# Adapter groups issued behind a quad's last product, and five steps of the start and of superblock 3 issued at other places

## What is computed

```python
scale = cond @ norm_w.T + 1.0
h = x * (scale[:, None, :] * rsqrt(mean(x * x) + 1e-6))
val, gate = split(h @ up_w.T, 2)                  # up_w 4096 x 512
h = val * gelu(gate)                              # exact gelu
y = act_quant(h) @ weight_quant(down_w).T         # 2048 -> 512, int8 steps per token
x = y + x
Wd_b = Wd + ((cond @ Wdd.T + bdd) * 0.1).reshape(B, 128, 512)
Wu_b = Wu + ((cond @ Wdu.T + bdu) * 0.1).reshape(B, 512, 128)
x = x + relu(x @ Wd_b.T + bd) @ Wu_b.T + bu
```

## Time and profile before

| | |
|---|---|
| median of 3 runs | 892.72 us (890.46 to 893.59) |
| profiled execution, its time | 893.21 us |
| its span, first to last instruction | 891.5 us |
| PE busy | 860.0 us, 96% |
| DVE, ACT, POOL busy | 68%, 43%, 8% |
| mean granted PE clock | 0.994 of full |
| DMA, mean | 206 GB/s |
| PE's share of the chain that ended last | 77%; DVE 8%, DMA 6%, ACT 3% |

### The profile page before, as it was taken

One profiled execution on the slowest core, in us unless ns is written; L12 is line 12 of the kernel. 1 busy time (PEld: TensorE's weight loads), 2 busy tenths in 40 slices (PEclk: granted clock), 3 DMA queues, 4 the chain that ended last, 5 costly groups with the idle time before them and its releaser, 6 DMA issues.

```text
span 891.5 us, 11928 instructions
## 1 busy us (share of the span) xinstructions
PE 860.0 (96%) x4026; PEld 375.0 (42%) x4026; DVE 607.7 (68%) x944; ACT 384.7 (43%) x630; POOL 70.2 (8%) x79
## 2 busy tenths in 40 slices
PE   6889999999999999999999999999999999999988
PEld 5233343344444434444434444444444444444433
DVE  5757667588888775546886664558885764435976
ACT  5467787566645452224545452215433332224000
POOL 0413123130200000000200000000200000001000
PEclk9989999999999999999999999999999999999999
DMA  9739887766779895547595585353546443432311
GB/s 351 271 128 305 312 304 227 285 217 215 267 262 329 295 322 195 201 147 254 204 319 199 201 297 179 123 175 99 176 130 202 143 163 121 146 112 71 141 71 71
DMA packets 64283, 183.50 MB, mean 206 GB/s; under 512 B 7008, under 2 KB 8032, under 8 KB 64224
## 3 DMA queue, kind: packets, MB, share of 16 engines
q1 hardware_dynamic: 63936, 182.48, 59.2%
q10 hardware_dynamic: 288, 0.26, 0.1%
HBM read 152.31 MB, written 29.36 MB: 204 GB/s over the span
## 4 chain that ended last, share of the span: by engine, by line
PE 77%; DVE 8%; DMA 6%; issue 3%; ACT 3%; SPq 1%; POOL 0%; DVEq 0%; ACTq 0%; POOLq 0%
PE aux_ps L1078 9%; PE b_ps L989 8%; PE b_ps L993 7%; PE b_ps L991 7%; PE aux_ps L1034 6%; PE a_ps L989 5%; PE a_ps L993 5%; PE a_ps L991 5%; DMA w_ring<-in_Wdd 5%; PE aux_ps L1140 3%; PE e_ps L989 3%; PE c_ps L989 3%; PE e_ps L991 3%; PE c_ps L993 3%; PE c_ps L991 3%
## 5 line engine op out<-in xcount | busy, mean ns | idle before, releaser
L786 ACT ACTIVATE b_ps<-a_ps 128x512 f32<-128x512 f32 x63 | 36.7, 582 | 178.9 <-PE a_ps L993 178.7
L1475 DVE SCALAR_TENSOR_TENSOR h_ring<-v_sb,unscale,gelu 128x512 f32<-128x512 f32 x63 | 48.6, 772 | 87.7 <-ACT gelu L810 55.2
L989 PE MATMUL b_ps<-t_mov,u_l 128*128 128x512 f16 x252 | 95.8, 380 | 2.1 <-DVE c_ps L1436 2.0
L993 PE MATMUL b_ps<-t_mov,u_l 128*128 128x512 f16 x252 | 95.5, 379 | 0.0
L991 PE MATMUL b_ps<-t_mov,u_l 128*128 128x512 f16 x252 | 95.5, 379 | 0.0
L1444 DVE TENSOR_TENSOR v_sb<-b_ps,p_sb 128x512 f32<-128x512 f32 x63 | 43.5, 690 | 66.0 <-PE b_ps L993 65.6
L1499 DVE TENSOR_TENSOR hmax<-gelu,hmax 128x512 f32<-128x512 f32 x120 | 82.4, 687 | 6.7 <-ACT gelu L816 1.1
L1078 PE MATMUL aux_ps<-h_ring,wq 128*128 128x512 f16 x384 | 84.8, 379 | 0.0
L1034 PE MATMUL aux_ps<-w_ring,cond_sb 128*32 128x512 f32 x480 | 69.2, 601 | 7.4 <-DMA w_ring<-in_Wdd 3.6
L681 POOL PARTITION_ALL_REDUCE yscale<-hmax x8 | 18.0, 2298 | 606.1 <-DVE hmax L1499 606.1
L820 ACT ACTIVATE gelu<-h_ring 128x512 f32<-128x512 f32 x64 | 40.3, 630 | 55.0 <-DVE h_ring L1475 55.0
(11 more groups left out here) (214 smaller groups left out, 1605.9 us busy)
## 6 DMA issues: line engine op xcount, KB each, us to landing
w_ring<-in_Wdu SPq DMA_DIRECT2D x64, 512.0 KB, 7.0
w_ring<-in_Wdd SPq DMA_DIRECT2D x56, 512.0 KB, 7.1
u_l<-ul_dram SPq DMA_DIRECT2D x48, 512.0 KB, 4.4
u_e<-ue_dram SPq DMA_DIRECT2D x48, 384.0 KB, 3.1
h_ring<-in_up_w SPq DMA_DIRECT2D x16, 512.0 KB, 6.9
x_sb<-in_x SPq DMA_DIRECT2D x8, 1024.0 KB, 8.4
res<-in_down_w SPq DMA_DIRECT2D x16, 512.0 KB, 6.0
ul_dram<-u_l SPq DMA_DIRECT2D x15, 512.0 KB, 7.8
```

Source lines behind the costliest of these rows:

```text
L989: pe.matmul(ps[:, :], weight(n, p, 0, k), hi, start=fresh and k == 0, stop=False, skip_group_check=True)
L993: mm = pe.matmul(ps[:, :], weight(n, p, 1, k), hi, start=False, stop=k == 1, skip_group_check=True)
L1475: dve.scalar_tensor_tensor(out=h_slot(n)[:, TB:TS], in0=val[:, :], scalar=unscale[:, s // 2, j:j + 1], in1=gelu2[:, :], op0=ALU.mult, op1= ...
```

## The change

Four things, none of which changes an operation; the same instructions are issued on each engine.

1. On PE the two adapter groups of a quad stand behind product 7, at the head of the side work.
2. In the start on DVE: `power(1)` directly behind `rsqrt(1)`, ahead of one low part of the weights, one of x and four `x_scaled`; the sum T4 ahead of `seed_c(1)` instead of behind `u_low(2, 0)`.
3. In the start on ACT: `u_high(1, 1)` and the copy of group 4 ahead of the high part of T3; the copies of groups 5, 6 and 7 each one step or more earlier; the row sums of chunk 4 at the end of the start instead of in the middle of quad 1.
4. In superblock 3 on DVE: `scales(3, 0)` in quad 50 ahead of `multiply2(49)` and `seed_c(50)`, instead of ahead of `val2(50)`.

```diff
--- before.py
+++ after.py
@@ -865,17 +865,18 @@
             t_high(0, T1)
             t_high(0, T2)
             u_high(1, 0)
+            u_high(1, 1)
+            stage_group(4)
             t_high(0, T3)
-            stage_group(4)
-            u_high(1, 1)
             gate2(0)
+            stage_group(5)
             u_high(1, 2)
+            stage_group(6)
             u_high(1, 3)
-            stage_group(5)
-            stage_group(6)
+            stage_group(7)
             absolute1(0)
             absolute2(0)
-            stage_group(7)
+            row_sums(4)
             for n in range(1, NQ):
                 s, j = divmod(n, NP)
                 last = j == NP - 1 and s + 1 < NSB
@@ -901,7 +902,7 @@
                     absolute2(n - 1)
                 if last:
                     t_high(s + 1, T2)
-                if s == 0 and j + 3 < NP:
+                if s == 0 and 1 < j and j + 3 < NP:
                     row_sums(j + 3)
                 if n > 1:
                     absolute1(n - 1)
@@ -1189,11 +1190,11 @@
                     if n > 1:
                         product(n - 1, 4)
                     product(n, 2)
-                    for g in groups_of_quad(n):
-                        adapter_group(g)
                     product(n, 7)
-                for key in side_work(n)[len(groups_of_quad(n)):]:
-                    if key[0] == "stat":
+                for key in side_work(n):
+                    if key[0] == "dw":
+                        adapter_group(key[1])
+                    elif key[0] == "stat":
                         stat(key[1])
                     elif key[0] == "rs":
                         spread_rs(key[1])
@@ -1615,10 +1616,10 @@
             x_scaled(0, (2, 3))
             mean_square(1)
             rsqrt(1)
+            power(1)
             u_low(0, 2)
             t_low(0, B21)
             x_scaled(1)
-            power(1)
             t_low(0, B12)
             t_low(0, B22)
             moving_sum(0, T1)
@@ -1635,6 +1636,7 @@
             t_low(0, T3)
             u_low(1, 2)
             u_low(1, 3)
+            moving_sum(0, T4)
             seed_c(1)
             running_max1(0)
             running_max2(0)
@@ -1671,6 +1673,8 @@
                         power(j + 2)
                     if j + 1 < NP:
                         u_low(j + 1, 0)
+                if s == NSB - 1 and j == 2:
+                    scales(s, 0)
                 if s > 0 and j in QUANTISE:
                     first = 1 + sum(v for q, v in QUANTISE.items() if q < j)
                     quantise(s - 1, range(first, first + QUANTISE[j]))
@@ -1679,9 +1683,7 @@
                 if last:
                     moving_sum(s + 1, T2)
                     t_low(s + 1, B11)
-                if n == 1:
-                    moving_sum(0, T4)
-                else:
+                if n > 1:
                     multiply2(n - 1)
                     seed_c(n)
                     multiply1(n - 1)
@@ -1698,8 +1700,10 @@
                     t_low(s, B22)
                 if j == 0 or n == 1:
                     t_low(s, T4)
-                if s > 0 and j in (1, 2):
-                    scales(s, 2 - j)
+                if s > 0 and j == 1:
+                    scales(s, 1)
+                if 0 < s < NSB - 1 and j == 2:
+                    scales(s, 0)
                 val2(n)
                 if n == 1:
                     sums_low(0)
```

## The result

| | before | after |
|---|---|---|
| median of the runs, us | 892.33 (888.31 to 893.59, 6 runs) | 877.18 (875.56 to 880.11, 6 runs) |
| profiled execution, us | 893.21 | 875.56 |
| its span, us | 891.5 | 873.8 |

The ratio is 0.984, 95% interval 0.9815 to 0.9866: the changed kernel is 1.6% faster. The prediction was 875.0 with a range of 870.5 to 883.5. The profiled pair shows 17.7 us.

The account below looks back on a forecast made before the run. PE's own matmuls bound the kernel; reordering returns only waits and lost clock. Start 8.5, superblock 0 6.0, quads 35 and 38 2.2, scales(3, 0) 1.3: 18.0 us off 893.2, given as 875, range 870.5 to 883.5.

Parts of the forecast that it names:

- The start, 8.5 forecast: Start to quad 3: reordered VectorE and ScalarE work makes quad 3 start about 9.2 us earlier, taken as 8.5.
- the wait for group 7's bank: Start: PE still waits 1.9 us for the copy of group 5, which frees that bank.
- the replay: Start recomputed at full clock from timeline durations: quad 3 starts near 65.3 to 66.3 us, against 75.21.
- The first rival: Start: the clock falls again behind remaining waits, up to 3.0 us of work lost, 877 to 878; chance 0.15.
- the sign that the clock is full from 24 us on: Start: listed among what would show the forecast right, full PE clock from 24 us on.
- Superblock 0, 6.0 forecast: Quads 4 to 14: product 7 runs during tile waits, 5 x 1.30 = 6.5 us, less 0.5 for bounds.
- the five quads of the forecast: Quads 4, 7, 9, 12 and 14 of superblock 0: each gains 1.30 us from groups behind product 7.
- a sign of being wrong: Groups behind product 7: the forecast is wrong if they still take 3 us there.
- Quads 35 and 38, 2.2 forecast: Tiles issued later behind a queue backlog land when they did, so the quads gain 0.93 + 1.30 = 2.2 us.
- scales(3, 0), 1.3 forecast: Quads 50 and 51: moved into VectorE's idle time, it removes product 7's seed wait in quad 51, 1.3 us.
- The spare of 0.5 in quad 17: Quad 17, second tightest: without the groups as cover, 0.5 us are left between seed end and product 7.
- The rival of a kernel that gets slower: 28 quads with groups: product 7 waits for a late seed, some 20 us lost or 903 us total; chance 0.03.

Follow-up runs that it names:

- the third part alone: Kernel before with only scales(3, 0) moved two products earlier: 889.46 us, ratio 0.9988 [0.9961, 1.0015].
- the late seed on before: Kernel before with multiply2 issued four times instead of once ahead of seed_c in twelve quads with groups: 897.76 us in its one run.
- the earlier issue: SyncE issues a quad's weight tiles one loop iteration earlier where the quad between has no groups: on the kernel before 887.74 us, on the changed kernel 874.12 us.
- the second part alone: Kernel before with only the adapter groups moved behind product 7, start and scales(3, 0) as before: 882.91 us, ratio 0.9905.
- the three kernels with other copies: Changed kernel with ScalarE's copies early and some groups in front: 877.44 us; with tiles also issued earlier 872.74; that at chosen quads only 874.22.
- the late seed: Changed kernel with multiply2 issued four times instead of once ahead of seed_c in twelve quads with groups: 888.65 us in its one run.

## Why the prediction was right, step by step

**The start, 8.5 forecast, 7.7 measured.** The mechanism held. Group 1 starts at 26.23 with no wait. The sum T3 runs from 40.03 to 41.24 (forecast: ends at 40.1). The seed's wait in quad 2 is 1.40 (1.6), that of the bounds 0.49 (0.4), and the wait for the row sums is gone. The mis-sized term is the wait for group 7's bank: 3.02, against 1.9. T3 ended 1.1 later than in the replay, and the copy that frees the bank stands behind T3's high part, which gives the difference. The replay took VectorE's durations from stretches in which GpSimd was idle; a later section shows what that missed. Quad 3 begins at 66.75 to 66.80 in the two traces of this start without a stretch at half the clock, and at 67.25 to 68.00 in the five with one; the replay had 65.3 to 66.3.

The first rival, the clock falling again, came true in part. It does so behind the wait of 3.02 and costs 0.7 in the profiled run, 0.5 to 1.2 over those traces; the rival had up to 3.0. So the sign that the clock is full from 24 us on failed. The median, 877.2, is the number of this rival (877 to 878), but not for its reason: the two of the six runs at a mean clock of 1.0 took 877.43 and 876.93, no less than the four at 0.998.

**How much of the 7.7 is clock.** The start of before, with no half-clock stretch (trace of the third part alone), reaches quad 3 at 71.69, and with the two of its own profile at 75.21. The changed start without one reaches it at 66.80. So the waits give 4.9, and the clock the other 2.8: 3.5 less 0.7. The forecast of 8.5 had the clock in it: it set a replay at full clock against a start that ran twice at half, and gave 3 us as the clock's part. The Trainium skill, TensorE: Matmul & The Clock Gate, Part 1, says that how many matmuls run slow at a kernel's start varies between runs of one kernel. These traces show such a difference later in the start too: quad 3 starts at 76.01, 75.21 and 71.69 in three traces whose code is the same up to there (the late seed on before, before, the third part alone).

**Superblock 0, 6.0 forecast, 7.7 in the pair.** Over the traces the forecast is the better number. Quads 4 to 15 take 143.5 to 145.8 in the six kernels with the groups in front and the old issue, 144.5 in the mean. They take 138.1, 139.3 and 139.6 in the three with the groups behind and the old issue, 139.0 in the mean: 5.6. The 2.64 of quad 9 was the accident of one pair. That 5.6 is so near 6.0 is luck in part. By these means the five quads of the forecast (4, 7, 9, 12, 14) give 0.70, 1.19, 1.44, 0.83 and 0.81, where it had 1.30 each and 0.5 off the sum: the surplus of 12 and 14 was larger in the one trace of before than in the others (quad 12 lasts 13.60 there, 13.11 in the mean). And quad 15 gives 0.60, where the forecast had nothing. Quad 9's groups still take 3.56 us behind product 7 (5.60 before), which the prediction had named as a sign of being wrong. It isn't one there, for that quad's surplus was 3.7, and 1.30 of it is all that product 7 can cover. That the issue of these tiles, and not PE's place, sets when they land is what the earlier issue showed.

**Quads 35 and 38, 2.2 forecast, 1.8 in the pair.** In front, these quads last 11.72 and 13.86 in the mean of seven kernels. Behind, they last 11.02 and 12.32 in three (the changed kernel, the second part alone, and the changed one with earlier tiles). That is 2.2; in the three kernels with other copies quad 38 lasts 11.94 to 12.16. The queue did as forecast: quad 38's tiles are issued 2.04 ahead of the quad's start in the seven and the last lands 10.0 to 11.8 behind it. In the changed kernel they are issued 0.73 ahead and the last lands 10.4 behind it.

**What the prediction missed: 0.9 lost in quads 25, 27, 28 and 41.** Behind the groups' later copies it looked at the next `seed_b` alone. In these quads a user of the auxiliary banks stands directly behind the groups. Quad 27 of the changed kernel, ScalarE's copy of the second group and TensorE's products of the quantised part behind the transposes:

```profile
348.38 0.60 ACT L831 ACTIVATE stage<-aux_ps 128x512 f32<-128x512 f32 x1 [0.26 <-PE aux_ps L1035]
```

```profile
348.24 0.65 PE L1067 MATMUL aux_ps<-ident,rs 128*128 128x128 f32 x4
349.03 2.33 PE L1079 MATMUL aux_ps<-h_ring,wq 128*128 128x512 f16 x10
```

The products start 0.79 behind the transposes, as the copy ends at 348.98; in the kernel before they start 0.44 behind them (363.53 to 363.97 in quad 27). The edit that put the groups back in front there returned all 0.9.

**scales(3, 0), 1.3 forecast, 1.4 measured**, and product 7 of quad 50 starts as before, as forecast.

**The seed.** The spare of 0.5 in quad 17 is confirmed: in the changed kernel the seed ends at 231.52 and product 7 starts without a wait at 232.01, from VectorE's and TensorE's timelines:

```profile
230.83 0.69 DVE L1437 TENSOR_TENSOR c_ps<-b_ps,p_sb 128x512 f32<-128x512 f32 x1
```

```profile
232.01 0.38 PE L990 MATMUL b_ps<-t_mov,u_l 128*128 128x512 f16 x1
```

The rival of a kernel that gets slower had the right mechanism: a seed later by more than the spare costs the surplus in every quad with groups, as the late seed showed. Its condition is not met here.

**The sum.** 18.0 against 17.7 in the profiled pair: the mis-sized terms (-0.8, +1.7, -0.4, -0.9, +0.1) cancel nearly. That is luck in part, and the 877.2 of the median is 2.2 above the forecast.

## What to carry to other kernels

Where an engine waits for a transfer, first look at what the issue of that transfer stands behind. Moving independent work into the wait gave back 5.6 us here in superblock 0, and issuing earlier as well 2 to 3 more. Every instruction moved behind another takes its successors' banks with it, so ask for each quad separately what comes next. And two executions of one kernel can differ by more than the edit: add up the edit's gain by the places where it should act, over several traces.

## What the runs showed of the hardware

**The clock of the start differs between runs of one kernel.** Fifty runs of the kernel before stand beside these experiments. In 30 of them the mean granted clock is 0.994 or lower, median 893.2; in 19 it is 0.997 or higher, median 889.8. Of the 27 runs with the whole changed start none is below 0.996. Against the 889.8 the changed kernel gains 12.6, not 15.2: 2 to 3 us of the measured gain is that the dearer case no longer comes. That the shorter waits are what keeps it away is not shown. A long wait is no sure cause of it: in the trace of the third part alone PE waits 3.35 ahead of group 1 (at 29.82), as before, and the clock stays full until quad 3.

**VectorE and GpSimd slow each other.** Two sums of VectorE and two of GpSimd's weight sums in the changed kernel, first VectorE's timeline (the sum T1 overlaps GpSimd, the sum T3 doesn't), then GpSimd's:

```profile
32.21 1.74 DVE L1417 TENSOR_TENSOR h_ring<-x_sb 128x1024 f32<-128x1024 f32 x1
...
40.03 1.21 DVE L1417 TENSOR_TENSOR h_ring<-x_sb 128x1024 f32<-128x1024 f32 x1
```

```profile
28.80 0.73 POOL L669 TENSOR_TENSOR yscale<-yscale,h_ring 128x256 f32<-128x256 f32 x1
...
31.17 1.70 POOL L673 TENSOR_TENSOR yscale<-h_ring,yscale 128x256 f32<-128x256 f32 x1
32.83 1.70 POOL L666 TENSOR_TENSOR h_ring<-h_ring 128x256 f32<-128x256 f32 x1
```

The same sum takes 1.74 beside GpSimd's work and 1.21 alone; GpSimd's step takes 1.70 instead of 0.73. The Trainium skill, SBUF — State Buffer, Who interferes with whom, says that a VectorE instruction with both inputs in SBUF contends with GpSimd's reads, and the trace agrees. In the kernel before T1 took 1.22, for GpSimd was then waiting. It isn't always both that lose: there T2 took 1.22 (from 38.45) beside a step of GpSimd that took 1.74 (from 38.52). The change moved VectorE's work beside GpSimd's, which cost 0.5 in each of the sums T1 and T2.
